# Group statistics and softmax rows by another way, multiplications of ones on TensorE, another order at both ends

## The reference

```
g   = groupnorm(x)                       # mean, variance over 12 channels x 1024 tokens
w   = g^T . qkv_w^T                      # [1024, 384], 12 heads x 32
wn  = w / max(norm of w over tokens, 1e-12)
s   = sum over the head's 32 channels of wn^2      # [12, 1024]
Pi  = softmax over the 12 heads of s * temp[head]  # [12, 1024]
dots = sum over tokens of (Pi / (sum over tokens of Pi + 1e-8)) * w^2
u   = -(w * Pi) / (1 + dots)
y   = x + (u . out_w^T + out_b)
```

## Time and profile before

| | |
|---|---|
| median of 3 runs | 917.19 us (916.14 to 918.69) |
| the profiled execution | 916.16 us, of which the span 914.3 |
| mean granted TensorE clock | 0.991 |
| TensorE busy | 878.0 us (96%), 4404 matmuls, 4404 weight loads |
| VectorE busy | 720.4 us (79%) |
| ScalarE busy | 541.5 us (59%) |
| GpSimd busy | 225.5 us (25%) |
| DMA | 154.39 MB, 169 GB/s over the span; 36836 packets |

### The profile page before, as it was taken

One profiled execution on the slowest core, in us unless ns is written; L12 is line 12 of the kernel. 1 busy time (PEld: TensorE's weight loads), 2 busy tenths in 40 slices (PEclk: granted clock), 3 DMA queues, 4 the chain that ended last, 5 costly groups with the idle time before them and its releaser, 6 DMA issues.

```text
span 914.3 us, 14405 instructions
## 1 busy us (share of the span) xinstructions
PE 878.0 (96%) x4404; PEld 691.1 (76%) x4404; DVE 720.4 (79%) x1366; ACT 541.5 (59%) x740; POOL 225.5 (25%) x101
## 2 busy tenths in 40 slices
PE   4699999999999999999999999999999999999976
PEld 3568777777877777877777787777787777778754
DVE  7478877888887787887788888878788778888654
ACT  3465656765566675565676555667556567655621
POOL 1122333212333321233321233332123332113300
PEclk9899999999999999999999999999999999999997
DMA  7125544445544345554445554434555444454331
GB/s 270 58 72 209 189 162 153 154 185 207 209 151 180 132 170 204 209 189 161 154 148 187 207 209 147 186 133 170 200 209 185 164 156 148 185 207 142 141 140 70
DMA packets 36836, 154.39 MB, mean 169 GB/s; under 512 B 4306, under 2 KB 7762, under 8 KB 32850
## 3 DMA queue, kind: packets, MB, share of 16 engines
q1 hardware_dynamic: 36672, 154.17, 46.7%
q10 hardware_dynamic: 146, 0.00, 0.0%
HBM read 102.24 MB, written 51.92 MB: 169 GB/s over the span
## 4 chain that ended last, share of the span: by engine, by line
PE 93%; DVE 3%; DMA 1%; issue 1%; ACT 1%; DVEq 0%; SPq 0%; ACTq 0%
PE acc L466 86%; PE scores L546 5%; PE scores L554 1%; DVE stats L626 1%; DMA PIB<-pi 1%; DVE WS L729 1%; PE small L454 0%; DMA X<-in_x 0%; PE small L460 0%; DVE XL L676 0%; DVE UL L765 0%; PE acc L443 0%; DVE X L773 0%; ACT XH L393 0%; DVE WV L755 0%
## 5 line engine op out<-in xcount | busy, mean ns | idle before, releaser
L317 POOL TENSOR_TENSOR XL<-XN,XH 128x1024 fp32r<-128x1024 f32 x93 | 222.5, 2408 | 623.3 <-ACT XH L393 623.3
L365 ACT ACTIVATE WS<-acc 128x1024 f32<-128x1024 f32 x96 | 98.7, 1028 | 275.0 <-PE acc L466 274.7
L466 PE MATMUL acc<-UH,W2H 128*128 128x512 f32 x576 | 181.4, 398 | 7.9 <-ACT UH L355 7.9
L773 DVE SCALAR_TENSOR_TENSOR X<-acc,bias,X 128x1024 f32<-128x1024 f32 x96 | 118.3, 1260 | 85.8 <-PE acc L466 85.8
L466 PE MATMUL acc<-XH,W1H 128*128 128x512 f32 x576 | 183.9, 401 | 2.0 <-ACT XH L393 2.0
L466 PE MATMUL acc<-XH,W1L 128*128 128x512 f32 x576 | 180.6, 395 | 0.0
L466 PE MATMUL acc<-UH,W2L 128*128 128x512 f32 x576 | 180.2, 396 | 0.0
L466 PE MATMUL acc<-UL,W2H 128*128 128x512 f32 x576 | 150.3, 396 | 0.0
L466 PE MATMUL acc<-XL,W1H 128*128 128x512 f32 x576 | 147.0, 390 | 0.5 <-POOL XL L317 0.5
L466 PEld LDWEIGHTS acc<-UL,W2H 128*128 128x128 f32 x576 | 105.7, 188 | 33.8 <-issue 12.8
L466 PEld LDWEIGHTS acc<-UH,W2H 128*128 128x128 f32 x576 | 106.5, 190 | 29.5 <-ACT UH L355 8.5
(11 more groups left out here) (74 smaller groups left out, 469.6 us busy)
## 6 DMA issues: line engine op xcount, KB each, us to landing
PIB<-pi SPq DMA_DIRECT2D x96, 516.0 KB, 6.3
out_y<-X SPq DMA_DIRECT2D x96, 512.0 KB, 7.4
X<-in_x SPq DMA_DIRECT2D x31, 1536.0 KB, 6.3
pi<-PIT SPq DMA_DIRECT2D x32, 48.4 KB, 1.6
X<-in_x SPq DMA_DIRECT2D x3, 512.0 KB, 4.8
WV<-in_L_conv_qkv_w SPq DMA_DIRECT2D x1, 576.0 KB, 6.7
WS<-in_L_conv_out_w SPq DMA_DIRECT2D x1, 576.0 KB, 7.7
temp_row<-in_L_conv_temp ACTq DMA_DIRECT2D x1, 0.0 KB
```

Of the source, the lines that this page charges most:

```text
L317: pool.tensor_tensor(XL[:, t, :], XN[:, t, :], XH[:, t, :].bitcast(F32), ALU.subtract).then_inc(xl_done, 1)
L365: act.activation(square_tile(i, t), acc[:, t, :], ACT.Square, accum_out=sumsq[:, t:t + 1]).then_inc(squared, 1)
L466: last = pe.matmul(out[:, h * BANK:(h + 1) * BANK], w[:, k, m * P:(m + 1) * P], r[:, k, h * BANK:(h + 1) * BANK], start=(n == 0 and k == 0 ...
L773: dve.scalar_tensor_tensor(x_tile(j, t), acc[:, t, :], bias[:, t:t + 1], x_tile(j, t), ALU.add, ALU.add).then_inc(y_done, 1)
```

## The change

Group statistics. For all images but the first, the two small matmuls, `group_spreads` and their PSUM columns are gone. SyncE writes `stats` (128 x 36) to DRAM and reads it back so that each of a group's four partitions has the group's 4 x 36 values (`gathered`); VectorE's `bn_aggr` over 144 values gives the group's mean and variance (`group_mv`). That aggregation stands where `group_spreads` stood. The first image keeps the matmuls, under a semaphore of its own, in another place of the order.

Softmax rows. PI is written to PSUM; VectorE transposes it in 32 x 32 blocks to PIT (128 x 3 x 33) and sums the rows. `turn_pi` on TensorE and `keep_pi` on ScalarE are gone. PIT goes to DRAM in three DMAs, one for a tile, each with its semaphore; rows are of 33 values, not 129, and so is PIB.

TensorE multiplies ones by ones, 6, 3, 4 and 24 times, into PSUM that nobody reads: behind the first small matmul, behind the turning of W1, behind the turning of W2, and ahead of the last product. ScalarE makes XH of image 0 between the casts of W1H and W2H. The last product goes by output tiles: upper terms of tile 0, of tile 1, low terms of 0, upper of 2, low of 1, low of 2. In the last step VectorE's finish of the image before stands behind the dot products, still ahead of the attention. The first image's moments stand ahead of the head masks.

```diff
-SM_SHIFTED, SM_STEPS = 3, 6
+IDLE_TURNS = (6, 3, 4, 24)
+SM_SHIFTED, SM_STEPS = 3, 8
...
+      def write_stats(j):
+        if has(j):
+          sp.wait_ge(gn_step, j.counts(GN_STEPS, GN_MEASURED))
+          if j.follows(2):
+            sp.wait_ge(stats_gathered, j.counts(16, -16))
+          sp.dma_start(stats_dram, stats[:].rearrange("p k s -> p (k s)")).then_inc(stats_written, 16)
...
+      def gather_stats(j):
+        if has(j):
+          sp.wait_ge(gn_step, j.counts(GN_STEPS, GN_AGGREGATED - GN_STEPS))
+          sp.wait_ge(stats_written, j.counts(16))
+          rows = stats_dram.rearrange("(g k) s -> g (k s)", k=PER_GROUP).unsqueeze(1)
+          sp.dma_start(gathered[:], rows.to_broadcast([GROUPS, PER_GROUP, PER_GROUP * T * HALVES * 6]))\
+            .then_inc(stats_gathered, 16)
...
-          sp.wait_ge(pi_kept, j.counts(1, 1))
-          sp.dma_start(pi_dram.rearrange("h (b n) -> (h b) n", n=P + 1), PIT[:]).then_inc(pi_written, 16)
-          sp.wait_ge(pi_written, j.counts(16, 16))
+          sp.wait_ge(sm_step, j.counts(SM_STEPS, SM_STEPS))
           for t in range(T):
-            heads = pi_dram[t * HPT:(t + 1) * HPT].unsqueeze(0).to_broadcast([D, HPT, BLOCKS * (P + 1)])
+            rows = pi_dram[t * HPT:(t + 1) * HPT].rearrange("h (b q n) -> q (h b) n", b=BLOCKS, q=QUADS)
+            sp.dma_start(rows, PIT[:, t, :]).then_inc(pi_written[t], 16)
+          for t in range(T):
+            sp.wait_ge(pi_written[t], j.counts(16, 16))
+            heads = pi_dram[t * HPT:(t + 1) * HPT].unsqueeze(0)\
+              .to_broadcast([D, HPT, BLOCKS * QUADS * (QUAD + 1)])
             sp.dma_start(PIB[:, t].rearrange("p b n -> p (b n)"), heads).then_inc(pi_spread[t], 16)
...
+        write_stats(i + 2)
         store(i - 1, 0)
         store(i - 1, 1)
+        gather_stats(i + 2)
+      write_stats(FIRST + 1)
+      gather_stats(FIRST + 1)
       pipeline(sp, step, 0, B + 1)
...
       group_seeds(FIRST)
-      for k in range(2 * T):
-        act.wait_ge(weights_turned, k + 1)
-        act.activation(W1H[:, k, :] if k < T else W2H[:, k - T, :], turned(k), ACT.Copy,
-                 scale=1.0 if k < T else -1.0).then_inc(weights_hi, 1)
+      def weights_higher(ks):
+        for k in ks:
+          act.wait_ge(weights_turned, k + 1)
+          act.activation(W1H[:, k, :] if k < T else W2H[:, k - T, :], turned(k), ACT.Copy,
...
-      pipeline(act, step, -1, B)
+      weights_higher(range(T))
+      step(FIRST - 1)
+      weights_higher(range(T, 2 * T))
+      pipeline(act, step, 0, B)
...
+      def idle_turns(into, count):
+        for _ in range(count):
+          pe.matmul(into, ones[:], ones[:], start=True, stop=True)
+      def first_group_means():
+        pe.wait_ge(groups_set, 2)
+        pe.wait_ge(first_gn, FIRST_AGGREGATED)
+        pe.matmul(small[:, 0:1], group_mean[:], part_mv[:, 0:1], start=True, stop=True).then_inc(first_gn, 1)
+      def first_group_variances():
+        pe.wait_ge(first_gn, FIRST_SPREAD)
+        pe.matmul(small[:, 1:2], group_mean[:], spread[:], start=True, stop=True).then_inc(first_gn, 1)
...
+        idle_turns(small[:, P:2 * P], IDLE_TURNS[3])
+        for t, ns in [(0, (0, 1)), (1, (0, 1)), (0, (2,)), (2, (0, 1)), (1, (2,)), (2, (2,))]:
+          if ns == (0, 1):
+            acc_left(j - 1, t)
+          for k in range(T):
+            for n in ns:
+              if t == 0 and n == 0:
+                pe.wait_ge(uh_done, j.counts(T, k + 1))
+              if t == 0 and n == 2:
+                pe.wait_ge(ul_done[k], j.counts(1, 1))
+              last = term(acc[:, t, :], t, (W2H, W2L), (UH, UL), n, k)
+          if ns == (2,):
+            last.then_inc(m2_done, 1)
...
         first_product(i, 0)
-        group_means(i + 1)
         first_product(i, 1)
         first_product(i, 2)
-        group_variances(i + 1)
         second_product(i - 1, 0, {(2, 0): lambda: head_sums(i)})
-        turn_at = (1, 1) if has(i + 1) else (0, 0)
-        second_product(i - 1, 1, {turn_at: lambda: turn_pi(i)})
+        second_product(i - 1, 1, {})
         second_product(i - 1, 2, {})
...
       pe.matmul(temp_ps, ones[0:1, :], temp_row[0:1, :], start=True, stop=True).then_inc(temp_spread, 1)
-      group_means(FIRST)
-      group_variances(FIRST)
+      idle_turns(acc[:, T - 1, 0:P], IDLE_TURNS[0])
+      first_group_means()
       pe.wait_ge(masks_step, 3)
       pe.wait_ge(w1_loaded, 16)
-      turn_weights(range(T))
+      turn_weights([0])
+      first_group_variances()
+      turn_weights(range(1, T))
+      idle_turns(acc[:, T - 1, 0:P], IDLE_TURNS[1])
       pe.wait_ge(w2_mixed, 1)
       pe.wait_ge(temp_kept, 1)
-      pe.wait_ge(gn_step, GN_STEPS)
+      pe.wait_ge(gn_step, GN_AGGREGATED)
       turn_weights(range(T, 2 * T))
+      idle_turns(acc[:, T - 1, 0:P], IDLE_TURNS[2])
       pe.wait_ge(weights_lo, T)
       pipeline(pe, step, 0, B)
...
+        dve.wait_ge(first_gn, FIRST_VARIANCES)
+        dve.tensor_copy(group_mv[:], small[:, 0:2]).then_inc(gn_step, 1)
       def group_moments(j):
-        if not has(j):
-          return
-        dve.wait_ge(gn_step, j.counts(GN_STEPS, GN_MEASURED))
-        dve.memset(wait_cell[:], 0.0)
-        dve.bn_aggr(part_mv[:], stats[:].rearrange("p k s -> p (k s)")).then_inc(gn_step, 1)
...
+        if has(j):
+          dve.wait_ge(stats_gathered, j.counts(16))
+          dve.memset(wait_cell[:], 0.0)
+          dve.bn_aggr(group_mv[:], gathered[:]).then_inc(gn_step, 1)
...
+        link(dve.tensor_tensor(PI.rearrange("p h b -> p b h"), EX,
+                     srec[:].unsqueeze(2).to_broadcast([P, BLOCKS, HEADS]), ALU.mult))
         if j.follows(1):
-          dve.wait_ge(pi_turned, j.counts(1))
-        link(dve.tensor_tensor(PI[:].rearrange("p h b -> p b h"), EX,
-                     srec[:].unsqueeze(2).to_broadcast([P, BLOCKS, HEADS]), ALU.mult),
-           follows=False)
+          for t in range(T):
+            dve.wait_ge(pi_written[t], j.counts(16))
+        link(dve.transpose(PIT[:, :, 0:QUAD], scores[:, P:P + HEADS * BLOCKS]))
+        link(dve.tensor_reduce(PIT[:, :, QUAD], PIT[:, :, 0:QUAD], AX_X, ALU.add), follows=False)
...
           dve.wait_ge(pi_spread[t], j.counts(16, 16))
           dve.wait_ge(squared, j.counts(T, t + 1))
           dve.wait_ge(scores_done, j.counts(1, 1))
-          dve.tensor_tensor_reduce(in_blocks(square_tile(j, t)), PIB[:, t, :, 0:P],
+          dve.tensor_tensor_reduce(in_blocks(square_tile(j, t)), PIB[:, t, :, 0:QUAD],
...
         if k > 0:
           dve.wait_ge(u_step, j.counts(U_STEPS, T + k))
         if k == 0:
-          done = dve.tensor_reduce(total, PIB[:, :, :, P], AX_X, ALU.add)
+          done = dve.tensor_reduce(total, PIB[:, :, :, QUAD], AX_X, ALU.add)
...
       def step(i):
-        finish(i - 2, 2)
+        if has(i) or not has(i - 1):
+          finish(i - 2, 2)
         for t in range(T):
           dot(i - 1, t)
+        if not has(i) and has(i - 1):
+          finish(i - 2, 2)
         for k in range(4):
           attention(i - 1, k)
-        group_spreads(i + 1)
+        group_moments(i + 1)
         weigh(i - 1, 0)
         weigh(i - 1, 1)
         weigh(i - 1, 2)
...
         softmax_shift(i)
         softmax_divide(i)
         group_stats(i + 2, range(1, T))
-        group_moments(i + 2)
         finish(i - 1, 0)
         finish(i - 1, 1)
...
...
+      first_group_moments()
...
+      head_columns(0)
+      first_group_spreads()
+      head_columns(1)
+      head_columns(2)
+      first_group_kept()
       dve.wait_ge(heads_set, T)
       dve.wait_ge(temp_spread, 1)
       at_channels(pick[:], temp_ps).then_inc(temp_kept, 1)
       dve.wait_ge(temp_kept, 1)
       dve.tensor_reduce(temp_o[:], pick[:], AX_X, ALU.add).then_inc(temp_kept, 1)
-      group_moments(FIRST)
-      group_spreads(FIRST)
       group_norm(FIRST)
       weights_lower(range(T))
       normalise_first()
```

More of the change, by code:

```diff
@@ L41 @@
 QUAD = 32
-(GN_MEASURED, GN_AGGREGATED, GN_MEANS, GN_OFFSET, GN_SPREAD, GN_VARIANCES, GN_LOGGED, GN_SEEDED, GN_SCALED, GN_RESIDUE,
- GN_ROOTED, GN_STEPS) = range(1, 13)
+(GN_MEASURED, GN_AGGREGATED, GN_LOGGED, GN_SEEDED, GN_SCALED, GN_RESIDUE, GN_ROOTED, GN_STEPS) = range(1, 9)
+FIRST_AGGREGATED, FIRST_MEANS, FIRST_OFFSET, FIRST_SPREAD, FIRST_VARIANCES = range(1, 6)
 HEADSUM_STEPS = 3
-SM_SHIFTED, SM_STEPS = 3, 6
+IDLE_TURNS = (6, 3, 4, 24)
+SM_SHIFTED, SM_STEPS = 3, 8
 ATTENDED = 3 + 4
@@ L127, in conv_attention @@
         wait_cell = sb("wait_cell", [P, 1])
+        gathered = sb("gathered", [P, PER_GROUP * T * HALVES * 6])
+        group_mv = sb("group_mv", [P, 2])
         part_mv = sb("part_mv", [P, 2])
@@ L147, in conv_attention @@
         srec = sb("srec", [P, BLOCKS])
-        PI = sb("PI", [P, HEADS, BLOCKS])
-        PIT = sb("PIT", [HEADS * BLOCKS, P + 1])
-        PIB = sb("PIB", [P, T, BLOCKS, P + 1])
+        PIT = sb("PIT", [P, T, QUAD + 1])
+        PIB = sb("PIB", [P, T, BLOCKS * QUADS, QUAD + 1])
         pick = sb("pick", [P, T, HEADS])
```

(40 more changed lines are left out.)

24 lines of the change are left out of this document (7 added, 17 removed).

## The result

The changed kernel takes 908.87 us (907.02 to 910.04, 4 runs) against 916.71 in the runs beside it: 0.9909 of the time, 95% interval 0.9885 to 0.9932. It is faster, as forecast, but by 8 us (0.9%) where I had forecast 24. The profiled execution took 909.34, span 907.6 (914.3 before).

What follows compares the result with a forecast made beforehand. TensorE, 93% of the span, was taken as the bound, with VectorE's ring hardly shorter. 914.3 - 12.5 (middle) - 7 (start) - 3 (end) = 891.8, plus 1.9 = 893.7; forecast 893 us, range 879 to 909.

Steps and rivals of the forecast that it cites:

- the ring: Middle: loop of VectorE's weighing, softmax, PI's DMAs and dot products; 25.9 us an image before, 26.6 forecast after, setting the period.
- (d): Middle, VectorE's wait for the next image's statistics gathered through DRAM: +0.2 us an image (0 to +0.6).
- (a): Middle, VectorE ahead of the weighing: offset and spread go, -0.44 us an image.
- (e): Middle, VectorE's aggregation reads 144 values, not 36, inside the ring: +0.6 us an image (0.31 to 1.25).
- (b): Middle, PI to its DMA: VectorE's transpose and sum replace the way over TensorE and ScalarE, -0.2 us an image.
- (c): Middle, PI's write to DRAM becomes three of shorter rows: +0.3 us (up to +1.0); spreads grow by +0.15.
- rival (B): PI's three writes run on few DMA engines: +0.9 instead of +0.3 us, period 27.2, time 912; chance 0.13.
- the 2.2 that I had named as the sign of being wrong: PI's DMAs: forecast wrong if the first spread starts more than 2.2 us after the first write.
- (f): Middle, VectorE: larger sums of PIB +0.07 us, shorter rows for dot and weigh +0.05; +0.1 in the sum.
- Start: First image: earlier XH and ones holding TensorE's clock bring the head sums to 31.4 from 39.04; -7 us taken.
- D's mechanism: Rival, both ends: the ones don't raise the clock, the ends give 3 us, not 10; time 900, chance 0.08.
- End: Last product: 24 ones keep the clock high, one finishing pass remains behind it; -3 us (-0.5 to -3.3).

Runs made afterwards that it cites:

- e_rows16: Changed kernel with each of PI's three writes going to 128 consecutive DRAM rows instead of four blocks of 32 (output not the reference's): 894.08 us, ratio 0.9755.
- e_late_ones42: Changed kernel with VectorE's aggregation moved behind the three weighings and 42 instead of 24 multiplications of ones ahead of the last product: 883.47 us, ratio 0.9643.

## Why the prediction was wrong, though its mechanism held

The mechanism was right: TensorE gives up 0.83 us an image, the ring takes its place, TensorE waits at the head sums for VectorE's weights. The bound named for TensorE, 26.2, is met (26.15). What failed is the size of the ring, 26.6 forecast, 27.04 measured; over 30 periods 13 us, nearly all that was missed. TensorE waits 0.8 us an image at the head sums, not 0.4, about all that it had given up. The step that failed is (d), the wait for the gather. The terms, from the stretch shown unless an average is named:

- (a), (e) offset and spread go, the aggregation comes: +0.28 where the two terms made +0.16. The aggregation takes 0.80, I took 0.6; (0.800 - 0.312) / 108 is 4.5 ns a value. The 0.73 worked out there was nearer than what I took.
- (b) PI's new way: from PI's end to the first write's issue 0.63 where I had 0.65, so this was right (the two passes take 0.28 and 0.25, 0.6 with what lies between); the pass that makes PI is 0.07 shorter as well, which makes the -0.32 of the table.
- (c) the first write: +0.52 where I took +0.3, by the shape (e_rows16). So rival (B), few engines, was true in kind; it had +0.9. The first spread starts 2.14 to 2.21 us after the first write, in all but one image just inside the 2.2 that I had named as the sign of being wrong. Spreads -0.06, I had +0.15.
- (d) the gather: the mis-sized term. I took 0.2 of wait, at most 0.6; it was 0.99 on average. Both sides were off. The gather lands 3.1 us after the last spread on average (2.9 in the stretch shown), where I had 2.4 to 3.0 and took 2.6. And I let VectorE reach the aggregation 2.4 after the spread's landing, as before, where it had come late to its last dot product; in the ring it starts that at once, and is there after 2.1.
- (f) larger sums and shorter rows: I took +0.1; the leg from the last dot product to the aggregation is 0.09 shorter, wait apart. The legs from the weighing to PI, where I had no change, are 0.19 shorter. What made these two shorter is not shown.

And I had built the remedy into the sentence on (d) without seeing it: behind the waiting aggregation stood three weighings that do not need it.

Start: -8.0 against -7. That the number came near is luck: I had it from ones that hold the clock, and without any ones it is the same (D's mechanism, for the start). The kernel before paid there in two ways. One is the low clock, which I had at 5.6 us for 11.2 us of busy time; 29 matmuls at the 0.2267 of the middle are 6.6 us, so it cost 4.6, and the granted clock's column doesn't show the first part of it (1.00 from 17.79 to 26, while pairs take 1.05). The other I had not read as a cost: TensorE stood for image 1's means, whose matmul stood in its order.

```profile
26.87 0.35 PE L454 MATMUL small<-part_mv,group_mean 128*128 128x1 f32 x2 [1.85 <-DVE part_mv L637]
```

With 1.45 for the first product's earlier start (16.34 against 17.79) these make 7.9 of the 8.0.

End: -0.7 against -3. From the last product on it was -1.3, with the clock low; the product itself started 0.6 later after the last head sums (20.9 against 20.3). I had said that it would stay put. The dot products end 0.8 sooner after the last head sums than before, although two of them waited for their spreads, but the finishing pass that was moved behind them now stands between them and the attention and takes 1.2:

```profile
878.30 1.23 DVE L752 CUSTOM_DVE_ANT_0 WS<-PIB,WS 128x1024 f32<-128x1024 f32 x1 [2.20 <-DMA PIB<-pi]
...
881.41 1.23 DVE L752 CUSTOM_DVE_ANT_0 WS<-PIB,WS 128x1024 f32<-128x1024 f32 x1 [1.88 <-DMA PIB<-pi]
...
883.84 1.28 DVE L796 SCALAR_TENSOR_TENSOR X<-acc,bias,X 128x1024 f32<-128x1024 f32 x1
```

TensorE was done with that pass's tile at 878.9. In its old place ahead of the dot products, the pass and the first of them would have been done by 881.2, before the second one's spread was there at 881.41. So the move cost up to 1.2 us by these rows, an estimate: no run has the pass in its old place with the rest of the change.

With the clock held, the stretch from the last product on goes from 20.4 to 17.4, the 3 us forecast. I had asked only whether the ones would last too long, not whether they would last long enough.

## What to carry to other kernels

When work leaves the bounding engine, add up the next ring leg by leg with its waits taken out, and take arrival times from the ring's own pace, not from an execution in which that engine had slack. Put an instruction that waits for a DMA behind the work that does not need it: one line moved was worth 23 us here. Multiplications that hold the clock have to reach until the product starts (42 did and gave 2.3 us, 24 did not and gave nothing); at the start here, where the new order left hardly an idle stretch, they were worth nothing.

## What the runs showed of the hardware

A DMA write to DRAM in four blocks of 32 rows of 132 B, the first of three, lets the DMA that waits for it start 2.16 us after its issue on average and makes 5 updates of its semaphore; one of the same rows in a single block 1.62 us and 16 updates (e_rows16). A transfer of 18 KB issued behind three of 528 KB on the same queue lands after 6.4 us (median). `bn_aggr` costs 0.31 us for 36 values and 0.80 for 144. With 4.30 us of idle time TensorE's clock was at 0.50 for the next 4.5 us; with 42 multiplications in place of 24, and so no idle stretch, it stayed at 1.00 (e_late_ones42).
